# A depthwise 3x3 convolution block on one NeuronCore: the four parts of TensorE's step in another order

## What is computed

```python
def _L0_conv_ref(x, w1, b1, fscale, conv_bias):      # x: normalized
    avg = x.mean(axis=(2, 3))
    dyn = avg @ w1.T + b1
    wk = sigmoid(dyn).reshape(b * c, 1, 3, 3)
    y = depthwise_conv(x, wk, padding=1) + conv_bias
    return (x - y) * fscale * x + y
out = x + _L0_conv_ref(_gn(x), ...)
```

## Time and profile before

| what | value |
|---|---|
| median of 3 executions | 283.49 us (282.74 to 284.69) |
| the profiled execution, its own time | 283.0 us |
| its span in the trace | 281.2 us (mean granted clock 0.976) |
| busy share of the span | PE 83%, DVE 84%, ACT 76%, POOL 81% |
| granted TensorE clock | full, except 46.1 to 52.9 us and 66.6 to 70.0 us, when it is half |

### The profile page before, as it was taken

How to read it: one execution, slowest core, us unless ns; L and a number is a source line. 1 busy time by engine, 2 the same in 40 slices (tenths; PEclk the granted TensorE clock), 3 DMA queues, 4 the chain that set the end, 5 groups by cost and what they waited for, 6 DMA issues and landing times.

```text
span 281.2 us, 9000 instructions
## 1 busy us (share of the span) xinstructions
PE 233.2 (83%) x3506; PEld 167.4 (60%) x3506; DVE 237.5 (84%) x569; ACT 213.3 (76%) x386; POOL 229.0 (81%) x258
## 2 busy tenths in 40 slices
PE   0038985996989899898989898989899898999991
PEld 0024773784757576665656674757576665767660
DVE  2647787797999999999999999999999999766655
ACT  2126875787797979798898979797979799899520
POOL 0053448859899999999999999999999999999883
PEclk9999997797999999999999999999999999999997
DMA  7999803198496969798796969696969744444466
GB/s 266 334 411 420 347 11 128 43 350 335 151 364 266 359 265 373 282 320 366 252 418 232 402 252 371 261 367 262 370 259 373 303 170 171 171 171 170 168 256 252
DMA packets 10371, 77.64 MB, mean 276 GB/s; under 512 B 1265, under 2 KB 1496, under 8 KB 2648
## 3 DMA queue, kind: packets, MB, share of 16 engines
q1 hardware_dynamic: 10328, 77.06, 70.6%
HBM read 39.31 MB, written 37.75 MB: 274 GB/s over the span
## 4 chain that ended last, share of the span: by engine, by line
PE 41%; DVE 32%; issue 15%; POOL 5%; DMA 4%; SPq 1%; DVEq 0%; ACT 0%; POOLq 0%; ACTq 0%
PE conv_ps L426 26%; DVE outs L576 14%; PE conv_ps L432 9%; DVE pieces L523 8%; DMA gates<-gate 4%; DVE taps L543 4%; DVE row_stats L530 3%; PE dyn_ps L412 3%; POOL outs L841 2%; DVE less_one L535 2%; POOL inv_std L798 1%; PE conv_ps L488 1%; PE stat_ps L405 1%; DVE taps L550 1%; SPq L314 1%
## 5 line engine op out<-in xcount | busy, mean ns | idle before, releaser
L426 PE MATMUL conv_ps<-xs,taps 64*64 64x448 f32 x1536 | 223.4, 554 | 17.6 <-DVE outs L576 14.0
L841 POOL TENSOR_TENSOR outs<-outs,linear 128x1152 f32<-128x1152 f32 x63 | 166.2, 2645 | 9.1 <-DVE outs L576 9.1
L426 PEld LDWEIGHTS conv_ps<-xs,taps 64*64 64x64 f32 x1536 | 102.6, 135 | 61.9 <-issue 47.6
L576 DVE SCALAR_TENSOR_TENSOR outs<-xs,beta,conv_ps 128x576 f32<-128x576 f32 x128 | 102.6, 803 | 28.4 <-PE conv_ps L426 28.3
L432 PE MATMUL conv_ps<-xs,taps 64*64 64x128 f32 x1536 | 119.4, 279 | 0.0
L713 ACT ACTIVATE linear<-xs,slope 128x576 f32<-128x576 f32 x128 | 109.4, 858 | 3.6 <-POOL outs L841 3.6
L523 DVE BATCH_NORM_STATS2 pieces<-xs 128x6 f32<-128x64 f32 (+1 forms) x256 | 102.4, 449 | 5.3 <-DMA xs<-x 5.3
L688 ACT ACTIVATE xs<-xs,shift 128x594 f32<-128x594 f32 x128 | 99.5, 781 | 0.0
L432 PEld LDWEIGHTS conv_ps<-xs,taps 64*64 64x64 f32 x1536 | 94.1, 136 | 2.5 <-issue 1.8
L798 POOL TENSOR_TENSOR inv_std<-numbers,minus_half 128x8 f32<-128x8 f32 x16 | 26.4, 1650 | 4.5 <-ACT dev_mean L694 4.4
L543 DVE TENSOR_TENSOR taps<-dyn_ps,tap 128x1512 f32<-128x1512 f32 (+1 forms) x19 | 27.8, 1477 | 0.0
(11 more groups left out here) (59 smaller groups left out, 138.0 us busy)
## 6 DMA issues: line engine op xcount, KB each, us to landing
xs<-x SPq DMA_DIRECT2D x30, 1188.0 KB, 11.2
out<-outs SPq DMA_DIRECT2D x30, 1152.0 KB, 5.6
xs<-x SPq DMA_DIRECT2D x4, 594.0 KB, 5.9
out<-outs SPq DMA_DIRECT2D x3, 576.0 KB, 3.1
out<-outs SPq DMA_DIRECT2D x2, 288.0 KB, 2.6
cst<-const SPq DMA_DIRECT2D x1, 248.0 KB, 7.3
w1s<-w1r SPq DMA_DIRECT2D x1, 115.9 KB
gates<-gate SPq DMA_DIRECT2D x1, 8.0 KB
```

The costliest lines, as they stand in the source:

```text
L426: return nc.tensor.matmul(tile(i, g, taken)[:, START:BANK], taps[given, i % 2, at:at + HALF], xs[given, i % XBUFS, g, 0:PAIRED, 1 + shift: ...
L576: nc.vector.scalar_tensor_tensor(out=outs[:, i % OBUFS, g].rearrange("p (k w) -> p k w", w=COLS), in0=xs[:, i % XBUFS, g, :, 1:1 + COLS], ...
L841: nc.gpsimd.tensor_tensor(tile, tile, linear[:, PAIR * k:PAIR * (k + 1)].rearrange("p g n -> p (g n)"), ALU.add).then_inc(out_ready, 1)
```

## The change

The step issues its four parts in another order: `across_first` of the tile, `own_parity` of the preceding tile, the odd place of the side chain, `across_second`, `own_halves`. No instruction is added or taken away, and no wait; SyncE, VectorE, ScalarE and GpSimd have the programs of before.

```diff
                 across_first(i, g)
-                own_halves(i, g)
+                if n > 0:
+                    own_parity(*tiles[n - 1])
                 chain(i, 2 * g + 1)
                 across_second(i, g)
-                if n > 0:
-                    own_parity(*tiles[n - 1])
+                own_halves(i, g)
             own_parity(*tiles[-1])
```

## The result

The kernel after takes 272.2 us (median of 4 executions, 272.12 to 272.44) against 283.69 (282.74 to 284.69) in the same job: 0.9596 of the time before, 95% interval 0.9562 to 0.963. The profiled execution took 272.44 us, span 270.7, and it is set against the one of before (283.0, span 281.2).

What follows compares the result with a forecast made beforehand. No engine was full; VectorE and TensorE waited on each other. Gains of 1.9 + 0.8 + 4.1 + 0.57 = 7.4 us took 283.0 to 275.6, forecast 276.0 as the median lies 0.5 above; range 272.5 to 283.

Steps and rivals of the forecast that it cites:

- Products without waits at tiles 0 and 1: Sign in steady images: VectorE's products at tiles 0 and 1 no longer wait for TensorE; these waits were 0.61 us a period.
- The margins of 0.08 to 0.3 us: Tiles 0 to 2 of steady images: time to spare before VectorE reaches each product, put at 0.1 to 0.3 us.
- the release that I put at 0.72 us: TensorE's step: own_parity can start 0.72 us after the tile's second crossing pass starts.
- own_halves last costs nothing: End of TensorE's step: own_halves queue beside across_second and the next across_first; 0 us, range -0.02 to +0.19 a step.
- The slower rival: TensorE's step: queued own_halves hold the next tile's across_first, 0.18 us a step; 287.3 us, chance 11%.
- Steady images: Images 3 to 13: the 21 waits of products for TensorE go but the margins; 6.2 us gained (4.0 to 6.4).
- GpSimd as the next limit: GpSimd's own period, 14.75 us against VectorE's 14.50, falls back 0.25 us an image and limits the gain.
- a sign against me: Steady images: VectorE waiting for GpSimd's tap before image 10 would show the forecast wrong.
- The start: Image 0 and the passage from image 1 to 2: 1.9 us (0.7 to 4) and 0.8 us gained.
- the sum: Whole kernel: gains of 1.9 + 0.8 + 4.1 + 0.57 = 7.4 us, where VectorE alone would gain 8.9.
- the tail: Last eight tiles: gain at most what GpSimd gains, 7.4 us; pace stays at the crossings' 1.50 us.
- The rival that said 272.5: GpSimd does not bind and the clock stays full at 47 us; 8.9 + 2 us gained, 272.5, chance 10%.

Runs made afterwards that it cites:

- e1: Kernel after with own_halves moved ahead of the side chain and across_second; 330.41 us, ratio 1.176.
- e8: Kernel after with GpSimd's adds over three quarters of each pair of tiles, the last quarter lacking its linear part; 267.09 us, ratio 0.946.
- e9: Kernel before with GpSimd's adds over three quarters of each pair of tiles; 280.67 us, ratio 0.997.
- The filled kernels: Kernels before or after with pairs of small matmuls added in TensorE's long waits of the start, so that the clock stays up; 270.84 to 280.96 us.
- e4: Kernel before with five pairs of small filling matmuls in image 0 and five ahead of image 2; 279.02 us, ratio 0.995.
- e7: Kernel after with four pairs of small filling matmuls in image 0 and two ahead of image 2; 270.84 us, ratio 0.960.
- e16: Kernel after with filling matmuls and tap made by VectorE instead of GpSimd, straight ahead of the weights; 302.95 us, ratio 1.084.
- e5: Kernel before with five pairs of small filling matmuls ahead of image 2 only; 280.96 us, ratio 0.994.
- e2: Kernel after with the side chain ahead of own_parity again; 272.6 us, ratio 0.972.
- e10: Kernel after with the side chain ahead of own_parity and GpSimd's adds over three quarters of each pair; 268.03 us, ratio 0.954.
- e3: Kernel before with own_parity moved just ahead of the side chain, own_halves staying straight behind across_first; 278.28 us, ratio 0.992.
- e14: Kernel after with two thirds of own_halves straight behind own_parity, the rest last; 304.19 us, ratio 1.082.
- e13: Kernel after with the first third of own_halves straight behind own_parity, the rest last; 278.11 us, ratio 0.990.
- e11: Kernel after with filling matmuls and tap moved from GpSimd to VectorE, one pair of statistics behind product 3; 274.47 us, ratio 0.977.
- e15: Kernel after with filling matmuls and tap made by VectorE instead of GpSimd, straight behind product 3; 270.43 us, ratio 0.967.

## Why the prediction was wrong

The direction and the mechanism held, point by point; the size did not.

- *Products without waits at tiles 0 and 1.* Right: none from image 3 to 12, one of 0.15 us at product 0 of image 2. The margins of 0.08 to 0.3 us were enough; the release that I put at 0.72 us behind a crossing pass's start takes 0.63 in e1 (305.84 to own_parity's weight load at 306.47).
- *own_halves last costs nothing.* Right, by a queue of four passes a quarter, where two waiting are what my estimate wanted. It is the part on which the change hangs: 1.50 us a tile in the tail, against 1.88 and 2.10 with two thirds or all of own_halves ahead of across_second. The slower rival (287.3) was right in kind, and its price of 0.18 us a step would have been far off: 0.6 where it decides.
- *Steady images.* 6.2 us forecast, 6.3 measured. Right for the wrong shares: the waits cost 0.81 us a period, not 0.61, and GpSimd, not VectorE, sets it from image 5 on.
- *GpSimd as the next limit.* Right and shown by e8 and e9. My 14.75 us was 0.18 too long, for its waits too cost more than the records say: ahead of the adds in one period of before stood 0.17 + 0.16 us, while without waits its records overlap by 0.04, and the moments began 0.38 us behind tap's start (168.25 to 168.63), 0.27 after (190.57 to 190.84). VectorE waited for tap from image 5 on, which I had named as a sign against me; it was small (0.17 us an image in the records), because its own path had shortened to 14.30 as well.
- *The start.* This is the step that failed. I costed image 0 and the passage to image 2 at the half clock of before ("Product 0 of image 2 depends on the crossings at half clock"), and gave the clock its place only in the upper end of one term ("0.7 to 4") and in one rival of 10%. "I count 0.8" for image 2 was 2.4; 1.9 for image 0 was 2.9. That is 2.6 us of the 3.3 by which 10.7 exceeds the sum's 7.4; the tail gave back 1.0 where the sum had 1.5, and the steady images 0.1 more. The filled kernels put 3.2 us on the clock (3.7 before less 0.5 after). At full clock in both (e4 less e7) the order brings 1.5 us in image 0, 0.9 in image 1, 6.1 to product 13.0, and gives back 1.0: 7.5 us from the first product to the last, where the sum had 7.4.

The rival that said 272.5 is nearest by its number, and by luck: its first condition, that GpSimd does not bind, fails in e8, and the clock did not stay at full (half from 47.6 to 51.0 us).

The trace of before could have warned me: both stretches of half clock begin within a wait of TensorE (2.97 and 2.28 us), and earlier products shorten both waits. TensorE's timeline of after has them at 1.88 and 1.53 us:

```profile
46.39 0.23 PE L370 MATMUL stat_ps<-moments,cst 64*64 64x16 f32 x2 [1.88 <-POOL moments L808]
...
63.97 1.34 PE L426 MATMUL conv_ps<-xs,taps 64*64 64x448 f32 x10 [1.53 <-DVE taps L550]
```

Half clock follows the first, from 47.6 us for 3.4 us, and not the second. That the clock falls about such waits is what these rows show, with e4 and e16; that a shorter wait is what keeps it up they do not show. In e5's profiled execution, which has the program of before up to image 1, TensorE stands the same 2.97 us in image 0 and the clock stays at full:

```profile
46.71 0.23 PE L370 MATMUL stat_ps<-moments,cst 64*64 64x16 f32 x2 [2.97 <-POOL moments L817]
```

Waits of 2.48 us in e2, 1.89 in e10, 1.97 in e8 and the first of 2.71 in e16 (to 79.45) left it at full too, while one of 1.94 in e3 and one of 2.37 in e9 have half clock with them. So what the order does to the clock, and how much of the 3.2 us was the turn of these executions, stays open. What is shown is that half clock cost that much where it came, and that the order brings 7.5 us without it.

## What to carry to other kernels

When a stretch of half clock lies about a wait of TensorE, give the clock's return a term and a chance of its own, not just the upper end of another term, and compare the two kernels at full clock as well: the same program has the stretch in one execution and not in the next, here 278.8 us or 284.6 by the mean clock. Read an engine's period from a stretch in which it has no wait; a period less the reported waits is too long (here by 0.2 us on two engines), as a wait also undoes the overlap of neighbouring instructions. And with separate quarters of the array, write down for each quarter what is still queued when the next instruction for another quarter is issued: with these f32 passes, a fifth for one of them stopped all.

## What the runs showed of the hardware

- **TensorE issues in order across quarters, four passes deep each** (64x64 quarters, f32). The tails of e1, e14 and e13, with eight, six and four passes a quarter (two of them own_parity's) ahead of across_second: 2.10, 1.88 and 1.50 us a tile; and e1's weight load at 307.51. The Trainium skill (TensorE: Matmul & The Clock Gate, section "The mechanism") has matmuls start and end in program order; within a quarter nothing here speaks against it, and across quarters do (own_halves from 159.14, the second pass of across_first, earlier in the program, at 159.53).
- **A VectorE instruction that reads two SBUF tensors is held by a GpSimd add that runs when it starts.** Tap takes 0.23 us free and 1.40 to 2.53 us when it starts well inside an add, ending 0.1 us after it (e11, e15, e16). The Trainium skill (GPSIMD Engine Reference, section "Specifications") states this contention for instructions with two SBUF inputs; by this rule, the traces agree. The products and the weights, which read one operand of PSUM, keep 0.8 and 1.7 us beside the same adds. It also stands in the tails of both kernels: after, `add_last` (L586) takes 1.78 us when it starts beside GpSimd's last add and 0.76 without one, and puts the last product off by 1.0 us:

```profile
264.71 1.78 DVE L586 TENSOR_TENSOR outs<-outs,linear 128x576 f32<-128x576 f32 x1
266.42 0.80 DVE L576 SCALAR_TENSOR_TENSOR outs<-xs,beta,conv_ps 128x576 f32<-128x576 f32 x1
267.25 0.76 DVE L586 TENSOR_TENSOR outs<-outs,linear 128x576 f32<-128x576 f32 x1
```

```profile
263.26 2.62 POOL L841 TENSOR_TENSOR outs<-outs,linear 128x1152 f32<-128x1152 f32 x1 [0.38 <-DVE outs L576]
```
